# A decoder's first stages on one core: attention in half batches, context norms by VectorE, distances pair by pair, skewing copies from three queues

## What is computed

```
x = x + L0_attn(layernorm(x))            # one head, causal, 112 x 112 scores per batch
x = x + L0_xattn(ctx, layernorm(x))      # alignment:
    D = sqrt(max(aa + bb - 2 * a @ b.T, 0))   # a: 112 rows of layernorm(x), b: 375 rows of ctx
    R[i, j] = D[i, j] + min(R[i-1, j], R[i, j-1], R[i-1, j-1])
    path = backtrack(R);  out = sum of the context rows that the path gives to each token
x = x + L0_ffn(...); x = x + L1_attn(...); x = x + L1_xattn(...); x = x + L1_ffn(...)
```

## Time and profile before

| | us |
|---|---|
| median of three executions | 635.02 (634.96 to 660.84) |
| the profiled execution | 631.45 |
| its span | 629.5 |
| TensorE busy | 472.0 (75%) |
| VectorE busy | 400.3 (64%) |
| ACT busy | 234.3 (37%) |
| POOL busy | 185.8 (30%) |

### The profile page before, as it was taken

One profiled execution on the slowest core, in us unless ns is written; L12 is line 12 of the kernel. 1 busy time (PEld: TensorE's weight loads), 2 busy tenths in 40 slices (PEclk: granted clock), 3 DMA queues, 4 the chain that ended last, 5 costly groups with the idle time before them and its releaser, 6 DMA issues.

```text
span 629.5 us, 9016 instructions
## 1 busy us (share of the span) xinstructions
PE 472.0 (75%) x2802; PEld 376.3 (60%) x2802; DVE 400.3 (64%) x1352; ACT 234.3 (37%) x670; POOL 185.8 (30%) x272
## 2 busy tenths in 40 slices
PE   6988999050002288699999996899999798799980
PEld 6974547040001035598899995778777475689850
DVE  6047765999989986453543257677874155756545
ACT  2357760030000421304344303389984545034300
POOL 6003260030000002135668324511102411366354
PEclk9988999675556599869999999999999999899995
DMA  5300111139410088712212140050005401045623
GB/s 169 116 24 1 37 28 24 37 55 149 72 16 0 10 269 274 163 26 68 69 55 72 50 134 1 2 169 1 2 2 156 145 1 59 27 135 167 136 85 115
DMA packets 48801, 49.07 MB, mean 78 GB/s; under 512 B 14656, under 2 KB 41908, under 8 KB 48532
## 3 DMA queue, kind: packets, MB, share of 16 engines
q1 hardware_dynamic: 40996, 33.37, 18.8%
q0 software_dynamic: 7760, 15.14, 10.2%
HBM read 36.14 MB, written 9.31 MB: 72 GB/s over the span
## 4 chain that ended last, share of the span: by engine, by line
PE 51%; DVE 28%; ACT 5%; issue 4%; SPq 4%; DMA 4%; POOL 2%; another core or an unknown queue 1%; DVEq 0%; ACTq 0%; POOLq 0%
PE ps L1143 45%; DVE big L1768 7%; PE ps L1146 6%; DVE mtmp L1763 4%; SPq L573 2%; DVE big L2118 1%; DVE rk L2110 1%; DVE big L1809 1%; DVE big L1810 1%; ACT N_r L921 1%; DVE big L1843 1%; SPq L569 1%; ACT big L893 1%; DMA big<-scattered 1%; DMA big<-in_L_attn_wo 1%
## 5 line engine op out<-in xcount | busy, mean ns | idle before, releaser
L1143 PE MATMUL ps<-ident 128*128 128x128 f32 (+1 forms) x304 | 63.2, 372 | 78.9 <-DVE big L1801 60.0
L1143 PEld LDWEIGHTS ps<-ident 128*128 128x128 f32 x304 | 46.0, 233 | 86.5 <-DVE big L1801 60.4
L1143 PE MATMUL ps<-ctxT_r,big 128*128 128x128 f32 (+1 forms) x616 | 83.2, 285 | 2.5 <-issue 1.2
L1143 PEld LDWEIGHTS ps<-ctxT_r,big 128*128 128x128 f32 (+1 forms) x616 | 75.8, 191 | 7.0 <-issue 5.0
L1768 DVE TENSOR_TENSOR_SCAN big<-mtmp,big 32x47 f32<-32x47 f32 x248 | 62.6, 287 | 11.6 <-DMA big<-Vc_r 11.6
L1143 PE MATMUL ps<-big 112*128 112x112 f32 (+6 forms) x458 | 61.6, 312 | 3.7 <-issue 3.4
L893 ACT ACTIVATE big<-ps 112x448 f32<-112x448 f32 (+5 forms) x63 | 38.4, 640 | 53.6 <-PE ps L1146 34.4
L1143 PEld LDWEIGHTS ps<-big 112*128 112x128 f32 (+5 forms) x458 | 51.7, 186 | 7.9 <-issue 4.3
L893 ACT ACTIVATE ctxT_r<-ps 128x256 f32<-128x256 f32 (+3 forms) x74 | 30.9, 433 | 60.5 <-PE ps L1146 34.6
L1146 PE MATMUL ps<-ident,big 112*112 112x112 f32 (+5 forms) x289 | 40.5, 277 | 13.4 <-DVE big L2118 4.4
L1146 PEld LDWEIGHTS ps<-ident,big 112*112 112x112 f32 (+5 forms) x289 | 30.5, 144 | 27.7 <-DVE big L1843 10.2
(11 more groups left out here) (269 smaller groups left out, 927.7 us busy)
## 6 DMA issues: line engine op xcount, KB each, us to landing
big<-in_L_ffn_W SPq DMA_DIRECT2D x16, 512.0 KB, 7.2
routed<-Vc_r SPq DMA_DIRECT2D x29, 128.0 KB
big<-in_ctx SPq DMA_DIRECT2D x4, 750.0 KB
ctxT_r<-in_ctx POOLq DMA_DIRECT2D x4, 750.0 KB, 20.5
big<-in_L_ffn_Wg SPq DMA_DIRECT2D x16, 128.0 KB, 2.4
big<-in_L_ffn_Wu SPq DMA_DIRECT2D x16, 128.0 KB, 2.5
big<-in_L_ffn_Wd SPq DMA_DIRECT2D x16, 128.0 KB, 2.5
normed<-N_r SPq DMA_DIRECT2D x2, 896.0 KB, 5.3
```

The lines of the kernel that those rows point to most:

```text
L1143: return nc.tensor.matmul(dst, lhsT, rhs, start=first, stop=last)
```

## The change

- **Half batches.** Queries and keys, values, scores, weights and the weighted sum go by halves of four batches, with pieces of the context's turning between them. The low parts of the weights are made in two instructions, and TensorE waits for each part where it uses it.
- **Norms of the context.** VectorE squares and sums each of the 24 context blocks as loaded (`ctx_squares`, 125 rows of 256, sum into a column of `aa`). TensorE turns twelve such columns at a time (`ctx_norms_turn`), and adds them in the distance bank: three matmuls per batch whose left side `sel` (12 rows, made by POOL) picks one column block. The copy of the turned token rows carries the factor -2, and the token norms, now squared and summed by ACT (`row_squares`), are the bias of the relu that empties the bank (`inverse_roots`). ones-matmuls, wide squares, `aaB`, and VectorE's additions are gone; `roots` keeps three instructions. One activation table is loaded at the start instead of two.
- **Pair by pair.** The distances of two batches at a time follow their layer norm, with the context's turning, the second half's weights and values between the pairs. ACT, which empties the distance banks, does relu, Ln and Exp of a pair in its own order.
- **Loads and copies.** SP loads context chunks 0 and 1, ACT chunks 2 and 3, after its first two bank copies. Of the skewing copies, block 0 is issued 15 by SP, 7 by ACT, 10 by POOL; block 1 12, 10 and 10; block 2 24 by SP and 8 by POOL. Each waits for its own pair.
- POOL's `ln_root(1)` no longer stands behind the last context turn, and its loads and clears wait for the things that now use the same places.

```diff
+        ln_slots[0] += ring.take(dve, dve)
+        r_qk0 += ring.take(*[act] * 4)
+        ln_slots[0] += ring.take(dve, dve)
+        r_v0 += ring.take(act, act)
+        r_s0 += ring.take(dve)
+        r_qk0 += ring.take(*[act] * 4)
+        r_pt0 += ring.take(dve)
+        r_ctx += ring.take(act, act)
+        r_pv0 += ring.take(dve, dve)
+        r_s0 += ring.take(dve)
+        r_v0 += ring.take(act, act)
+        r_ctx += ring.take(act, act)
+        r_aat += ring.take(act)
+        (turn1[0],) = ring.take(act)
+        r_dist += ring.take(act, act)
+        r_ctx += ring.take(act, act)
+        r_pt0 += ring.take(dve)
+        (turn1[1],) = ring.take(act)
+        r_ctx += ring.take(act, act)
+        r_pv0 += ring.take(dve, dve)
+        r_dist += ring.take(act, act)
+        r_ctx += ring.take(*[act] * 4)
+        r_aat += ring.take(act)
...
+        def mover(b, g, k):
+
+            if g == G - 1:
+                return "pool"
+            if k == 0:
+                return {4: "act", 5: "act", 7: ("act", "pool", "pool")[g]}.get(b, "sp")
+            if k == 1:
+                return ("sp", "sp" if b < HB else "act", "act" if b < B - 2 else "pool")[g]
+            return "sp"
+
+        def moved_by(queue, k):
+            return [(b, g) for b in range(B) for g in range(G) if mover(b, g, k) == queue]
+
+        def rows_in(k):
+
+            n = len(moved_by("pool", k))
+            return 16 * (G * B - n), 16 * n
...
-            for i in range(4):
+            for i in range(2):
                 sp.dma_start(ctxN0[:, 6 * i:6 * i + 6, :].rearrange("p (b c) d -> p b c d", c=CH),
                              c_d[:, 2 * i:2 * i + 2]).then_inc(ctx_loaded[i], 16)
...
+            for k in range(NBLK):
+                for b, g in moved_by("sp", k):
+                    sp.wait_ge(s["dist_ready"], b // 2 + 1)
+                    sp.dma_start(skewed(b, g, k), plain_rows(b, g, k)).then_inc(rows_moved[k], 16)
...
+            pool.wait_ge(s["ctx_squared"], BC)
...
+            for k in range(NBLK):
+                for b, g in moved_by("pool", k):
+                    pool.wait_ge(s["dist_ready"], b // 2 + 1)
+                    pool.dma_start(skewed(b, g, k), plain_rows(b, g, k)).then_inc(pool_rows_moved[k], 16)
...
+            for i in range(2, 4):
+                sc.dma_start(ctxN0[:, 6 * i:6 * i + 6, :].rearrange("p (b c) d -> p b c d", c=CH),
+                             c_d[:, 2 * i:2 * i + 2]).then_inc(ctx_loaded[i], 16)
...
+            def row_squares(q4):
+                for b in (2 * q4, 2 * q4 + 1):
+                    sc.wait_ge(s["norm_ready"], B + b + 1)
+                    nc.scalar.activation(root[:, b, 0:D], N[:, b, :], ACT.Square, accum_out=bb[:, b:b + 1])\
+                        .then_inc(s["bb_ready"], 1)
+
+            def inverse_roots(q4):
+                sl = slice(2 * q4, 2 * q4 + 2)
+                sc.wait_ge(s["bb_ready"], 2 * q4 + 2)
+                for b in (2 * q4, 2 * q4 + 1):
+                    copy(r_dist[b], Dd[:, b, :], bank(r_dist[b])[0:T, 0:S], ACT.Relu, bias=bb[:, b:b + 1])
+                sc.wait_ge(free[act], r_dist[2 * q4 + 1].count)
+                link(nc.scalar.activation(inv[:, sl, :], Dd[:, sl, :], ACT.Ln, bias=tiny[:, 0:1]))
+                nc.scalar.activation(inv[:, sl, :], inv[:, sl, :], ACT.Exp, scale=-0.5).then_inc(s["inv_ready"], 1)
+
+            qk_moved(0, 0, 4)
+            ln_hi(0, NTs_0, (1,))
+            v_moved(0)
+            qk_moved(1, 0, 1)
+            exp_rows(0, 0, 2)
+            qk_moved(1, 1, 2)
+            exp_rows(0, 2, 4)
+            qk_moved(1, 2, 4)
+            ctx_turned(0, 2)
+            v_moved(1)
+            ctx_turned(2, 4)
+            norms_turned(0)
+            pair_turned(turn1[0], 0, scale=-2.0)
+            row_squares(0)
+            exp_rows(1, 0, 4)
+            inverse_roots(0)
+            ctx_turned(4, 6)
+            pair_turned(turn1[1], 1, scale=-2.0)
+            row_squares(1)
+            ctx_turned(6, 8)
+            inverse_roots(1)
+            ctx_turned(8, 12)
+            norms_turned(1)
             copy(r_bias, bcol[:, :], bank(r_bias)[:, 0:NB])
-
-
-            def squares(q):
-                if q >= 2:
-                    sc.wait_ge(full, r_aa[q - 2].n + 1)
-                if q == 0:
-                    sc.wait_ge(free[act], r_ctx[-1].count)
-                nc.scalar.activation(csq[:, q % 2], ctxT[:, :, q * TC:(q + 1) * TC], ACT.Square)\
-                    .then_inc(s["csq_ready"], 1)
-
-            def norms(q):
-                lo = q * TC
-                copy(r_aa[q], Vc_r[0:T, B * S + lo:B * S + lo + TC], bank(r_aa[q])[0:T, 0:TC])
-            squares(0)
-            squares(1)
-            for q in range(AA_CUT):
-                norms(q)
-                squares(q + 2)
-            ln_turned(1)
-            for q in range(AA_CUT, NQ):
-                norms(q)
-
-            sc.wait_ge(s["consts_ready"], 5)
-            for q4 in range(B // 2):
-                sl = slice(2 * q4, 2 * q4 + 2)
-                sc.wait_ge(s["ln_arg"], q4 + 1)
-                link(nc.scalar.activation(inv[:, sl, :], Dd[:, sl, :], ACT.Relu))
-                link(nc.scalar.activation(inv[:, sl, :], inv[:, sl, :], ACT.Ln, bias=tiny[:, 0:1]))
-                link(nc.scalar.activation(inv[:, sl, :], inv[:, sl, :], ACT.Exp, scale=-0.5))
-                nc.scalar.activation(aaB[:, sl, :], inv[:, sl, :], ACT.Square).then_inc(s["inv_ready"], 1)
+            pair_turned(turn1[2], 2, scale=-2.0)
+            row_squares(2)
+            inverse_roots(2)
+            pair_turned(turn1[3], 3, scale=-2.0)
+            row_squares(3)
+            inverse_roots(3)
...
+            sc.wait_ge(s["dsk_clear"], 1)
+            for k in range(2):
+                for b, g in moved_by("act", k):
+                    sc.wait_ge(s["dist_ready"], b // 2 + 1)
+                    sc.dma_start(skewed(b, g, k), plain_rows(b, g, k)).then_inc(rows_moved[k], 16)
...
+            def distances(q4):
+
+                pe.wait_ge(s["sel_ready"], 1)
+                wait_act(r_ctx[KD * (((2 * q4 + 2) * S - 1) // TC) + KD - 1])
+                wait_act(r_aat[q4 // 2])
+                dst = [bank(r_dist[b])[0:T, 0:S] for b in (2 * q4, 2 * q4 + 1)]
+                for j in range(2):
+                    for c in range(CH):
+                        mm(dst[j][:, c * CR:(c + 1) * CR], sel[:, (2 * (q4 % 2) + j) * CH + c, :], aaT[:, q4 // 2, :],
+                           c == 0, False)
+                wait_act(turn1[q4])
+                for j in range(2):
+                    b = 2 * q4 + j
                     for k in range(KD):
-                        last = mm(dst[0:T, 0:TC], ones[:, :], csq[:, q % 2, k, :], k == 0, k == KD - 1)
+                        last = mm(dst[j], NT[:, k, tok(b)], ctxT[:, k, b * S:(b + 1) * S], False, k == KD - 1)
                     filled(last)
...
+            ln_turn(0, (0,))
+            query_key(0)
+            ln_turn(0, (1,))
+            values(0)
+            self_scores(0)
+            query_key(1)
+            weights_turned(0)
+            ctx_turn(0, 2)
+            self_values(0)
+            self_scores(1)
+            values(1)
+            ctx_turn(2, 4)
+            ctx_norms_turn(0)
+            pair_turn(turn1[0], 1, 0)
+            distances(0)
+            ctx_turn(4, 6)
+            weights_turned(1)
+            pair_turn(turn1[1], 1, 1)
+            ctx_turn(6, 8)
+            self_values(1)
+            distances(1)
+            ctx_turn(8, 12)
+            ctx_norms_turn(1)
             pe.wait_ge(s["aux_loaded"], 48)
             filled(turn(bank(r_bias)[:, 0:NB], brow, NB))
-            pe.wait_ge(s["consts_ready"], 1)
-            norms(0, AA_CUT)
-            ln_turn(1)
-            norms(AA_CUT, NQ)
-
-            wait_act(ln_slots[1][-1])
-            for b, slot in enumerate(r_dist):
-                dst = bank(slot)[0:T, 0:S]
-                for k in range(KD):
-                    last = mm(dst, NT[:, k, tok(b)], ctxT[:, k, b * S:(b + 1) * S], k == 0, k == KD - 1)
-                filled(last)
+            pair_turn(turn1[2], 1, 2)
+            distances(2)
+            pair_turn(turn1[3], 1, 3)
+            distances(3)
...
+            def ctx_squares(lo, hi):
+
+                for j in range(lo, hi):
+                    ve.wait_ge(ctx_loaded[j // 6], 16)
+                    if j >= 2:
+                        ve.wait_ge(s["ctx_squared"], j - 1)
+                    v.scalar_tensor_tensor(csq[:, j % 2], ctxN0[:, j, :], 1.0, ctxN0[:, j, :], ALU.mult, ALU.mult,
+                                           accum_out=aa[:, j:j + 1]).then_inc(s["ctx_squared"], 1)
...
+            weights_low(0, 2)
+            norm_lo_from_bank(0, NTs_0, (0,))
+            ln_norm(0, 3)
+            weights_low(2, 3)
+            ctx_squares(0, 6)
+            norm_lo_from_bank(0, NTs_0, (1,))
+            ctx_squares(6, 8)
+            ve.wait_ge(s["mask_ready"], 1)
```

(39 more changed lines are left out.)

286 lines of the change are left out of this document (126 added, 160 removed).

## The result

| | before | after |
|---|---|---|
| median of all executions | 634.99 | 626.83 |
| median of the undisturbed ones | 634.96 | 625.89 |
| span of the profiled execution | 629.5 | 620.8 |
| column 1 starts | 91.06 | 87.75 |
| idle ahead of column 17 | 6.40 | 1.56 |

The ratio is 0.985 with a 95% interval of [0.9814, 0.9886]: faster by 8.2 us by the medians of all, half of the forecast 16.4. "Undisturbed", here and in the ratios, leaves out the executions that took over 1.5% longer than the fastest of their kernel. Two later sets with the same kernel gave 0.9824 [0.9771, 0.9877] and 0.9893 [0.9845, 0.9941].

What follows compares the result with a forecast made beforehand. Bound by a chain of waits, from 91.06 us VectorE's alignment with two DMA holes: column 1 10.0 us earlier plus the 6.40 us hole gone gives −16.4, from 635.02 to 618.6; range 608 to 627.

Steps and rivals of the forecast that it cites:

- less comes: Rival: ACT's context chunks served first, chunk 1 lands at 34.5 (+4.6), 12-row matmuls cost 0.33 (+2.4): 625.6; chance 0.19.
- a whole second hole: VectorE's 6.40 us idle after alignment column 16 stays open in full: 618.6 + 6.4 = 625.0.
- Faster: Whole kernel: chance 0.78 of a gain that a measurement can tell from no change, about 2% (12.7 us).
- The context's arrival: Context loads: queues take turns, chunk 1 lands at 29.9 instead of 21.2; half 0's scores ready at 32.4, weights at 34.5.
- context in time: Rival: chunk 1 is there at 21 to 24, TensorE never stands, −8.3, 610.3; chance 0.27.
- The new front up to pair 2: TensorE's work from 34.5 through the distance pairs: 32.5 in all, a pair 3.94, waits for ACT 3.7.
- The clock: TensorE's idle from 29 to 34.5 brings a half-speed stretch: +1.5, and 0.3 for the transposes ahead.
- From the last distance to the fourth pair: After 72.5: hand-over, relu, Ln, Exp 2.5, then three VectorE steps of 0.95, ending at 77.9 against 85.75.
- The row copies, column 1: Skewing copies after the fourth pair: column 1 starts 3.2 later, at 81.1, 10.0 us earlier than before.
- with 2.8 to spare: Block 1's copies land at 89.3, column 17 needs them at 92.1, so the 6.40 us idle is gone.
- signs of being right: VectorE and TensorE idle for context, fourth pair at 75 to 80, no idle at column 17, later stages shifted equally.
- ScalarE's row issues: Rival: row copies on ACT's queue cost 6.1 each, 656.4; slower by 2% from 4.9; chance 0.04.

Runs made afterwards that it cites:

- ctx_sp: The changed kernel with all four context chunks issued by SP and none by ACT: median 620.82, ratio to the kernel before 0.9763.
- ctx16: The changed kernel with each context chunk loaded by two DMAs, of 112 and 13 partitions: median 617.82, ratio to the kernel before 0.9728.
- sqlate: The changed kernel with VectorE's squares of context chunk 1 behind the first scores and weights: median 620.22, ratio to the kernel before 0.9779.
- warm2: Second set of the changed kernel with ten unread matmuls in TensorE's waits before pairs 2 and 3: median 622.38, ratio to the kernel before 0.9864.
- poollate: The changed kernel with POOL issuing its block 2 copies only once block 1 has landed: median 621.33, ratio to the kernel before 0.9793.

## Why the prediction was right, and its gain twice too large

The median was forecast at 618.6 and came at 626.83, 8.2 later. That is inside the range of 608 to 627 by 0.2 us only, and outside the forecast's own 614 to 623. It lies by the numbers of the rival "less comes" (625.6, or 625.0 with a whole second hole), but not by its causes: chunk 1 landed as forecast, and 1.56 us of the hole stayed, not 6.4. "Faster" had 0.78, and a ratio of 0.985 is not beyond the 2% that the prediction set as the least that can be told. So the range holds partly by luck. By the prediction's own steps, in the profile:

- **The context's arrival**: right. Chunk 1 at 30.27 (29.9), scores of half 0 at 32.45 (32.4), weights turned at 34.56 (34.5). The 1.5 us that it put between an issue and its engines has no row of its own; the shortest landing in these traces is 1.6. ScalarE's second issue took 7.52 instead of 4.6, hidden as said. The rival "context in time" had the price of avoiding this delay about right: 8.3, where ctx_sp gave 6.0 and ctx16 9.0.
- **The new front up to pair 2**: right within 1.0: pair 2's first matmul was due at 62.97 (72.5 less its 3.94, 0.45, 1.2 and 3.94) and began at 63.94. Six 12-row matmuls took 1.50 against 1.38. Most of the 1.0 is clock: the work behind the idle of 5.5 us took 2.66 + 4.89 us where sqlate has 1.40 + 3.52, so 2.6 were lost and not 1.8.
- **The clock**: the mis-sized term. The step "The clock" priced one idle, that of 5.5 us, at 1.8, and took the waits before pairs 2 and 3 as waits only. The work behind them ran at half speed too: 4.8 more by warm2. The two pairs at full clock are another 0.7 over the sum (8.58 against 7.88). The last distance ended at 78.60, not 72.5.
- **From the last distance to the fourth pair**: 83.95 − 78.60 = 5.35, forecast 5.4.
- **The row copies, column 1**: 3.80 after the fourth pair, not 3.2. The prediction took SP's third copy for the last; it was issued at 85.16 and landed 2.3 later. POOL's fourth, at 0.49 an issue, was issued at 85.72 and landed 2.0 later, at the 87.7 at which column 1 starts: 0.6.
- **Column 17**: the step "with 2.8 to spare" failed. SP's last issue of block 1 began 8.9 us after the fourth pair, as worked out (9.0), but its copy took 7.54 to land, not the 2.4 of the earlier trace rows. That 2.4 is a median over 24 copies. Those issued beside POOL's block 2 took up to 7.6 in the trace of before already, and the change moved the last copy among them. Of the 5.1 us more, the 2.8 to spare and the late column 1 took up all but 1.6; poollate removed those.

Column 1 came 6.65 late and the hole kept 1.56: 8.2. So two of its signs of being right did not come: the fourth pair at 75 to 80 (83.95), and no idle at column 17. Of the rivals, ScalarE's row issues are refuted by the trace (median 601 ns, longest 674, against the 4.9 us from which they would have decided); nothing after the alignment failed to shift.

## What to carry to other kernels

When work is cut into finer pieces, price each new wait of TensorE twice: once for the wait, and once for the work behind it at half clock, which came here in nine profiles of ten. Before a load is moved to a second queue, read the DMA share: here it stayed at 0.34 with the second queue and the first transfer came late, while partition counts that spread wider (112 + 13 for 125) tripled it. An in-order engine should meet a late input after the work that others wait for. And a landing time is read by stretches: a median over all copies of a kind hid those that shared the engines with another queue's, and the change moved the one that mattered among them.
